# Norm factors of the combine stage as two float32r pieces, spread by one float32r product over 40 rows

## What is computed

```
x = _from_tokens(t, x)                    # t: tokens plus output of the first experts
x = x + _L1_conv_ref(_ln_c(x), w, b)      # 3x3 convolution, bias, relu, of the channel norm of x
t = _to_tokens(x)
t = t + _L1_ffn_ref(_ln_t(t), ...)        # graph attention and gated experts of the token norm

def _ln_c(v, eps=1e-06):                  # and _ln_t, over the last axis, with eps=1e-05
    m = jnp.mean(v, axis=1, keepdims=True)
    s = jnp.var(v, axis=1, keepdims=True)
    return (v - m) / jnp.sqrt(s + eps)
```

## Time and profile before

| | |
|---|---|
| median of 3 runs | 8130.51 us (8129.3, 8130.51, 8148.41) |
| profiled execution | 8119.96 us, of which the span is 8118.2 us |
| PE busy / PEld / DVE / ACT / POOL over the span | 7127.6 / 5237.2 / 5290.3 / 2133.9 / 5031.3 us |
| combine stage | from 2254 us (its first DVE instruction) to 3347 us (its last PE product) |
| mean granted clock of PE | 0.949 |

### The profile page before, as it was taken

How to read it: one execution, slowest core, us unless ns; L and a number is a source line. 1 busy time by engine, 2 the same in 40 slices (tenths; PEclk the granted TensorE clock), 3 DMA queues, 4 the chain that set the end, 5 groups by cost and what they waited for, 6 DMA issues and landing times. The chain is left out here.

```text
span 8118.2 us, 97223 instructions
## 1 busy us (share of the span) xinstructions
PE 7127.6 (88%) x34853; PEld 5237.2 (65%) x34853; DVE 5290.3 (65%) x7812; ACT 2133.9 (26%) x4196; POOL 5031.3 (62%) x4822
## 2 busy tenths in 40 slices
PE   8887888699959999489999999999999999999668
PEld 5666666466624444267777777777777777777457
DVE  6666656477765443167777777777777677777588
ACT  5555665344412121011111111111111111111110
POOL 2343333577735553477777777777777777777473
PEclk9998999799979999799999999999999999999889
DMA  7111111222133343551111211111111121111257
GB/s 188 55 59 53 49 49 69 83 59 58 41 100 88 86 71 46 58 62 42 42 42 41 50 45 42 42 42 42 42 42 41 44 50 42 42 42 42 80 190 271
DMA packets 464347, 533.44 MB, mean 66 GB/s; under 512 B 243520, under 2 KB 386302, under 8 KB 441346
## 3 DMA queue, kind: packets, MB, share of 16 engines
q1 hardware_dynamic: 295202, 327.93, 15.2%
q0 software_dynamic: 149632, 72.60, 7.0%
q10 hardware_dynamic: 19296, 130.03, 4.0%
HBM read 263.12 MB, written 278.84 MB: 67 GB/s over the span
## 5 line engine op out<-in xcount | busy, mean ns | idle before, releaser
L1870 POOL DMA_INDIRECT e_row<-rows_dram,e_idx x3328 | 3164.3, 951 | 1022.5 <-issue 1013.9
L1765 PE MATMUL e_found<-e_pieces,e_hot 128*128 128x512 f32 x12288 | 3043.8, 400 | 0.0
L1765 PEld LDWEIGHTS e_found<-e_pieces,e_hot 128*128 128x128 f32 x12288 | 2245.7, 188 | 498.4
L1902 DVE TENSOR_TENSOR e_hot<-e_spread,e_lows 128x1024 fp32r<-128x1024 f32 x770 | 935.2, 1215 | 300.5 <-PE e_spread L1751 293.9
L1927 DVE TENSOR_TENSOR e_prod<-e_found,e_pick 128x512 f32<-128x512 f32 x768 | 530.2, 690 | 799.8 <-PE e_found L1765 794.4
L1835 ACT ACTIVATE e_ex<-e_dx 128x512 f32<-128x512 f32 x64 | 38.5, 601 | 2936.2 <-DVEq L1963 2936.2
L1932 DVE TENSOR_REDUCE e_row<-e_prod 128x16 f32<-128x512 f32 x768 | 785.3, 1023 | 0.0
L1778 PE MATMUL e_bank<-e_h,e_w 128*128 128x512 f32 x1024 | 521.0, 634 | 176.4 <-ACT e_hid L1825 176.4
L799 POOL DMA_INDIRECT yb_dram<-b_y,b_home x320 | 547.6, 1711 | 206.8 <-issue 103.9
L309 POOL COPY a_xr<-a_xp 128x1573 f32<-128x1573 f32 x104 | 208.4, 2009 | 701.3 <-DVE a_xp L593 404.6
L1787 PEld LDWEIGHTS e_bank<-e_w,e_hid 128*128 128x128 f32 x4096 | 498.7, 195 | 101.0 <-issue 101.0
(11 more groups left out here) (393 smaller groups left out, 10008.2 us busy)
## 6 DMA issues: line engine op xcount, KB each, us to landing
ys_dram<-e_y ACTq DMA_DIRECT2D x64, 1024.0 KB, 3.9
f_ye<-ys_dram SPq DMA_DIRECT2D x64, 1024.0 KB, 6.2
e_row<-rows_dram,e_idx POOLq DMA_INDIRECT x3328
res_dram<-e_st ACTq DMA_DIRECT2D x64, 768.0 KB
xb_dram<-a_blanks SPq DMA_DIRECT2D x8, 2580.0 KB
b_tok<-xb_dram SPq DMA_DIRECT2D x80, 258.0 KB, 2.8
a_xr<-in_x SPq DMA_DIRECT2D x8, 2048.0 KB, 9.3
a_xs<-in_x SPq DMA_DIRECT2D x8, 2048.0 KB, 8.2
```

Source lines behind the costliest of these rows:

```text
L1765: mm = nc.tensor.matmul(found[k % 2][:].rearrange("p s c -> p (s c)"), hot[:, k % 2, g], pieces[:, q, g].rearrange("p s c -> p (s c)"), st ...
L1870: nc.gpsimd.indirect_dma_start(row[:, s, u], None, rows, bass.IndirectOffsetOnAxis(ap=idx[:, s, u:u + 1], axis=0)).then_inc(gath[s], 16)
L1902: nc.vector.tensor_tensor(hot[:, k % 2], spread[:].unsqueeze(1).broadcast_to([P, HG, P]), lows[:].unsqueeze(2).broadcast_to([P, HG, P]), A ...
```

## The change

The factors are no longer spread by an f32 product. After the reciprocal, DVE cuts each factor into a part with the lowest 12 bits cleared and a remainder, both held as float32r: the first in rows 0 to 7 of a 40-row tile, the second in rows 32 to 39. A constant tile `select` with ones at row c and row 32 + c of column c replaces the identity, so that one float32r product over 40 rows spreads the sum of the two parts.

```diff
-        rstdc, rstdt = sb("rstdc", [P, NT]), sb("rstdt", [P, NT])
+        R = mybir.dt.float32r
+        LOW = 32
+        rstdc, rstdt = sb("rstdc", [LT, 2, NT]), sb("rstdt", [LT, 2, NT])
+        piecec, piecet = sb("piecec", [LOW + LT, NT], R), sb("piecet", [LOW + LT, NT], R)
+        select = sb("select", [LOW + LT, LT], R)
...
-            for n, (t, value) in enumerate(((xp, 0.0), (eps6, 1e-6), (eps5, 1e-5), (zero, 0.0), (rstdc, 0.0),
-                                            (rstdt, 0.0))):
+            for n, (t, value) in enumerate(((xp, 0.0), (eps6, 1e-6), (eps5, 1e-5), (zero, 0.0))):
...
-                    nc.tensor.matmul(bank[:], ident[:, c:c + 1].broadcast_to([P, P]), rstd[:], start=True, stop=True).then_inc(sem_, 1)
+                    nc.tensor.matmul(bank[:], select[:, c:c + 1].broadcast_to([LOW + LT, P]), rstd[:], start=True,
+                                     stop=True).then_inc(sem_, 1)
...
+            def inverse(rstd, piece, i, spread, ready):
+
+                def part(ins):
+                    n_parted[0] += 1
+                    ins.then_inc(parted, 1)
+                    dve.wait_ge(parted, n_parted[0])
+
+                part(nc.vector.reciprocal(rstd[:, 0], rstd[:, 0]))
+                part(nc.vector.tensor_scalar(rstd[:, 1].bitcast(I32), rstd[:, 0].bitcast(I32), -(1 << 12), None,
+                                             ALU.bitwise_and))
+                if i:
+                    dve.wait_ge(spread, LT * i)
+                nc.vector.tensor_copy(piece[0:LT], rstd[:, 1])
+                nc.vector.tensor_tensor(piece[LOW:LOW + LT], rstd[:, 0], rstd[:, 1], ALU.subtract).then_inc(ready, 1)
...
+            nc.vector.memset(sqc[:], 0.0).then_inc(blanked, 1)
+            dve.wait_ge(blanked, 1)
+            for piece in (piecec, piecet):
+                nc.vector.tensor_copy(piece[:], sqc[0:LOW + LT, 0])
+            nc.vector.tensor_copy(select[:], sqc[0:LOW + LT, 0, 0:LT]).then_inc(blanked, 1)
+            dve.wait_ge(blanked, 2)
+            for low in (0, LOW):
+                nc.vector.tensor_copy(select[low:low + LT], ident[0:LT, 0:LT]).then_inc(blanked, 1)
...
-                    nc.vector.reciprocal(rstdc[0:LT], rstdc[0:LT]).then_inc(rstd_c, 1)
+                    i = rstd_c_at(g)[0]
+                    dve.wait_ge(dev_c, i + 1)
+                    inverse(rstdc, piecec, i, factor_c, rstd_c)
```

More of the change, by code:

```diff
@@ L989, in combine_conv_sort @@
         eps6, eps5 = sb("eps6", [P, 1]), sb("eps5", [P, 1])
-        consts, setup, setup_v = sem("consts"), sem("setup"), sem("setup_v")
+        consts, setup, setup_v, blanked = sem("consts"), sem("setup"), sem("setup_v"), sem("blanked")
+        parted = sem("parted")
         x1_loaded = [[sem(f"x1_loaded{z}{q}") for q in range(PAIRS)] for z in range(2)]
@@ L1239, in factors @@
                     bank = take("pm", emptied, LT * i + c + 1)
-                    nc.tensor.matmul(bank[:], ident[:, c:c + 1].broadcast_to([P, P]), rstd[:], start=True, stop=True).then_inc(sem_, 1)
-            pe.wait_ge(setup, 6)
+                    nc.tensor.matmul(bank[:], select[:, c:c + 1].broadcast_to([LOW + LT, P]), rstd[:], start=True,
+                                     stop=True).then_inc(sem_, 1)
+            pe.wait_ge(setup, 4)
             pe.wait_ge(consts, 80)
@@ L1271, in _ @@
                 if norm_c_at(g):
-                    factors(*norm_c_at(g), rstd_c, rstdc, normed_c, factor_c)
+                    factors(*norm_c_at(g), rstd_c, piecec, normed_c, factor_c)
                 if norm_t_at(g):
-                    factors(*norm_t_at(g), rstd_t, rstdt, normed_t, factor_t)
+                    factors(*norm_t_at(g), rstd_t, piecet, normed_t, factor_t)
                 if add_at(g):
@@ L1325, in centred @@
                     nc.scalar.activation(sq[:, c % 2], b[:], ACT.Square).then_inc(squared, 1)
-            act.wait_ge(setup, 6)
+            act.wait_ge(setup, 4)
             act.wait_ge(consts, 80)
@@ L1341, in _ @@
                         act.wait_ge(factor_c, LT * i)
-                    nc.scalar.activation(rstdc[0:LT], pvc[0:LT, :], ACT.Sqrt, bias=eps6[0:LT]).then_inc(dev_c, 1)
+                    nc.scalar.activation(rstdc[:, 0], pvc[0:LT, :], ACT.Sqrt, bias=eps6[0:LT]).then_inc(dev_c, 1)
                 if rstd_t_at(g):
@@ L1347, in _ @@
                         act.wait_ge(factor_t, LT * i)
-                    nc.scalar.activation(rstdt[0:LT], pvt[0:LT, :], ACT.Sqrt, bias=eps5[0:LT]).then_inc(dev_t, 1)
+                    nc.scalar.activation(rstdt[:, 0], pvt[0:LT, :], ACT.Sqrt, bias=eps5[0:LT]).then_inc(dev_t, 1)
                 for t in turn_slot.get(g, ()):
@@ L1430, in sort_step @@
                     state["stage"] += 1
+            n_parted = [0]
+            def inverse(rstd, piece, i, spread, ready):
[10 more added lines that the diff above has]
+                nc.vector.tensor_tensor(piece[LOW:LOW + LT], rstd[:, 0], rstd[:, 1], ALU.subtract).then_inc(ready, 1)
             n_rank = [0]
@@ L1458, in _ @@
             nc.vector.memset(frst[:, NTL:], float(NEDGE))
-            dve.wait_ge(setup, 6)
+            dve.wait_ge(setup, 4)
+            nc.vector.memset(sqc[:], 0.0).then_inc(blanked, 1)
[6 more added lines that the diff above has]
+                nc.vector.tensor_copy(select[low:low + LT], ident[0:LT, 0:LT]).then_inc(blanked, 1)
             nc.vector.tensor_scalar(cmat[:], ident[:], -1.0 / P, None, ALU.add).then_inc(setup_v, 1)
@@ L1478, in _ @@
                 if rstd_c_at(g):
-                    dve.wait_ge(dev_c, rstd_c_at(g)[0] + 1)
-                    nc.vector.reciprocal(rstdc[0:LT], rstdc[0:LT]).then_inc(rstd_c, 1)
+                    i = rstd_c_at(g)[0]
+                    dve.wait_ge(dev_c, i + 1)
+                    inverse(rstdc, piecec, i, factor_c, rstd_c)
                 if rstd_t_at(g):
-                    dve.wait_ge(dev_t, rstd_t_at(g)[0] + 1)
-                    nc.vector.reciprocal(rstdt[0:LT], rstdt[0:LT]).then_inc(rstd_t, 1)
+                    i = rstd_t_at(g)[0]
+                    dve.wait_ge(dev_t, i + 1)
+                    inverse(rstdt, piecet, i, factor_t, rstd_t)
                 if norm_c_at(g):
```

## The result

| | before | after |
|---|---|---|
| median, first comparison | 8134.35 us (9 runs) | 8159.96 us (9 runs, 8148.05 to 8165.97), ratio 1.0030, interval 1.0021 to 1.0040 |
| median, on another chip | 8129.47 us (13 runs) | 8160.65 us (4 runs), ratio 1.0044, interval 1.0027 to 1.0061 |
| span of the profiled run | 8118.2 us | 8157.5 us |
| combine stage, start of the first product of the convolution to start of the last table product | 2369.4 to 3347.1, 977.7 us | 2372.5 to 3377.1, 1004.6 us |
| falls of the clock (stretches at 1.2 GHz) in the stage from 2400 us on, ahead of its tail | 6, 41 us in all | 12, 113 us in all |

The changed kernel is 26 to 31 us slower, at the 0.3% that was called the bound of what can be told, and on the second chip more likely beyond it; both intervals lie above 1. The forecast of no change, 8132, is 28 us too low.

The account below looks back on a forecast made before the run. PE sets the pace, but its ring of banks ties it to DVE. Gains of 22.3 us less losses of 15.1 leave 7.2; the clock takes 9.2, so 2 us slower: 8132 on the median's scale, range 8100 to 8160.

Parts of the forecast that it names:

- The ring: Banks of `pm` that DVE frees for PE; PE waits 25.4 us in 13 places, which limits what shorter products gain.
- the clock: Slot 6: a wait of 6.6 us puts two more of six slots at long half clock, 9.2 us lost.
- the sum: Whole kernel: 7.2 us gained, 9.2 lost, so 2 us slower than the profiled 8119.96; 8132.5 on the median's scale.
- T: Start of a slot's first factor product, the end of the convolution before; DVE's times are fixed from there.
- Rival 1: The whole PE saving arrives, 79 us less the 3.9 at the start: 8055; chance 8%, cases between included.
- The price of the product: Factor products on PE: a pair takes 0.48 us instead of 1.72, saving 1.24 a pair, 79 us of PE work.
- The three instructions: DVE behind each reciprocal, three instructions of 8x512: 1.6 us, ends 1.2 and 10; 9.6 us lost in slot 6.
- Rivals 3 and 4: DVE's three instructions cost 10 us: 8200, chance 4%; the float32r product takes two records as f32: 8155, chance 3%.
- The start: Set-up on DVE, a memset, two casts and three tiny ones: 2.3 us; with the first 1.6, 3.9 us lost.
- The tail: End of the stage, factor products after the last reciprocal: 3 us gained, between 1.6 lost and 4.5 gained.
- Rival 2: Slot 6: the clock stays at half through the whole convolution, 42 us slower, 8172; chance 6%.
- all six long, the end of the stage without gain: Slow end of the range: all six slots 6 at long half clock, instructions at 2.1 us: 20 us lost, 8150.

Follow-up runs that it names:

- the product alone: Changed kernel with the factor as one float32r piece written by the reciprocal, without the three instructions behind it, remainder left out: 8111.29 us, ratio 0.9989 to the kernel before.
- the instructions alone: Kernel before with only the three DVE instructions added behind each reciprocal, results unused, product still f32: 8155.68 us, ratio 1.0023.
- both moves: Channel reciprocal behind token multiplications on DVE, variances and tables right behind first factors on PE: changed kernel 8043.16 us, ratio 0.9895; kernel before 8062.38, 0.9929.

## Why the prediction was right, and where it was wrong

The ring and the prices were foretold well, the clock was not. That the time stayed in the range is luck: the sum missed 28 of the 30 us, and without the 10 us by which the range was widened for the scatter of the runs the time would lie outside it. Two of the prediction's own signs of being right failed: PE is busy for 17 us less instead of 75, and the stage is 27 us longer, where 15 were allowed.

- **What bounds a slot: right.** DVE's multiplication is fixed by the convolution before. The centre starts 2.26 us after T in slots 0 to 2 and 4 (2.36 foretold) and 7.23 in slot 6 (7.16 foretold), with a wait of 6.50 (6.6). That 2.26 is under the 2.3 that was named as a sign of being wrong comes from T: the 40-row product is recorded later behind the convolution, and slot 3, which has no such product but ends at one, is 0.09 longer. Slot 7 wins 0.62 or 0.63 in the four images without a fall there. Of the PE time saved, 3.3 + 9.1 + 2.5 = 14.9 us arrived in the slots that no fall touched. Rival 1 falls with the experiment on the product alone.
- **The price of the product: a little off.** The pair takes 0.65 us, not 0.48, and slot 5 wins 1.06, not 1.24. The row that I took the price from has 128 rows, and with 128 rows the slot does win 1.25. I had called the number of rows unknown and put the bounds at 0 and 1.72, which hold it.
- **The three instructions: right.** 1.70 us for 1.6. Rivals 3 and 4 fall: each product is one record.
- **The start: 2.2 us short.** The set-up costs 2284.89 - 2282.41 = 2.5 us at the first cleaning of rows, near the 2.3 foretold. The rest of the 6.1 belongs to the first slots and was not traced further.
- **The clock: the step that failed.** Its sign was right, its place too narrow. I let the clock fall in slot 6 alone and counted two more long slots, 9.2 us. Slot 6 has three more (five of six are long), and where a slot goes from short to long it loses 6.1 to 6.5 us (1.6 + 4.6 = 6.2 foretold). All in all slot 6 lost 5.3 more than the sum says. The greater part lies where the sum had no clock at all: in slot 7 of image 0 a centre and a variance group behind a wait of 4.53 us run at half speed (+4.7 for 1.6), and in slots 4 and 7 and in the last image the clock falls five times at waits of 0.35 to 1.55 us behind short products (2.9, 3.2 and 1.7 more than foretold).
- **The tail: wrong in its sign.** The clock does not come back before the stage ends; every table group takes 3.61 us, where the first two took 1.86 before, and 3 us won became 3.2 lost, though the products there are short. The wait ahead of it grew from 4.14 to 5.95 us, but that is not what keeps the clock down: the product alone has the old wait and the same fall, the instructions alone have 5.84 us and a clock that comes back. In all nine profiles with a float32r product, of 40 rows or 128, it stays down; in all four with f32 it is back after 3.4 to 6.8 us.
- **The sum.** 28 us were missed in the stage: 5.3 in slot 6, 6.2 in the tail, 3.1 in slot 7 of image 0, 2.2 at the start, 7.8 in slots 4, 7 and the last image's falls, 2.1 by the dearer pair in slot 5 and the last image, and 1.1 in slots 0 to 2. Slots 0 and 1 win 0.16 each with 40 rows and with 128, so it isn't the price of the pair there; the two centres behind the wait take 1.89 us (2606.04 - 2604.15) instead of 1.81. All but the last two and the start are mostly falls of the clock. Rival 2, a clock at half through the whole convolution, did not happen, though 10.76 us for the convolution instead of 7.97 is part of the way.

What made the forecast uncertain was seen and bounded too tightly: "all six long, the end of the stage without gain" gave 20 us, and I put no term there for falls in other slots. What stays open is why the clock falls behind the short products without a wait, and why it stays down in the tail; with both moves 128 rows take away all the falls that had no wait, twice as many products some, and with neither does the clock come back in the tail.

## What to carry to other kernels

Where one engine is busy and yet paced by a ring of buffers, shortening its work turns into waits; ask first which instruction of the other engine the ring waits for, and move what stands ahead of it. Here moving one reciprocal behind two multiplications was worth 33 us with no product changed, and the shorter product began to pay only when its waits had other work in them. And cost a shorter TensorE instruction with the clock of all the slots in which it stands, not only of the one with the longest wait.

## What the runs showed of the hardware

- A float32r product of 512 columns over 40 rows costs more in a stream than one over 128 rows, 0.19 us a pair behind a convolution, though its own record is shorter (0.73 for 1.03 us a pair).
- The clock fell with PE busy throughout, behind a pair of 40-row float32r products and a group of 24-column tables, in five of six slots 6 with both moves; in none of the six with 128 rows (11.88 us each) or with f32 products in the same order (12.95 us each).
- At the end of the stage, behind a wait of 4.14 to 5.95 us, the clock came back after 3.4 to 6.8 us in the four profiles with f32 factor products, and not before the end of the stage in the nine with float32r ones.
- On DVE a reciprocal of 8x512 takes 3.33 us, beside 0.42 for a mask, 0.41 for a cast and 0.68 for a subtraction of the same shape.
